# A decoder layer on one Trainium2 core: where the down weights are rounded, where the shared product is added, when the partition maximum is taken

## What is computed

```python
x = x + attn(layernorm(x))            # 16 heads of 32; int8 activations, ternary weights, causal softmax
x = x + xattn(layernorm(x))           # part two, below
x = x + ffn(layernorm(x))             # part two as well

# xattn, 32 heads of 8 positions; v = layernorm(x), x1 = x2 = context
kv  = v[:, :, i] * x2[:, :, j]        # an 8 x 8 outer product for every channel l
y   = causal_convolution(kv, k) + kv * skip          # along l = 512
out = sum over i of y[i, j] * x1[i]

# ffn, inner size 1536, weights rounded to float8 (e4m3) and back
fuse = silu((x @ q(gate_w)) * gate_scale) * ((x @ q(up_w)) * up_scale)
y    = (fuse @ q(down_w)) * down_scale
```

## Time and profile before

| | us |
|---|---|
| median of 3 runs | 1605.58 |
| their lowest and highest | 1601.24, 1606.38 |
| the profiled execution, its own time | 1601.21 |
| span of its trace, first to last instruction | 1599.4 |
| PE, DVE, POOL, ACT busy in the span | 1479.1, 1261.7, 992.7, 697.4 |

### The profile page before, as it was taken

How to read it: one execution, slowest core, us unless ns; L and a number is a source line. 1 busy time by engine, 2 the same in 40 slices (tenths; PEclk the granted TensorE clock), 3 DMA queues, 4 the chain that set the end, 5 groups by cost and what they waited for, 6 DMA issues and landing times.

```text
span 1599.4 us, 23982 instructions
## 1 busy us (share of the span) xinstructions
PE 1479.1 (92%) x8967; PEld 839.6 (52%) x9045; DVE 1261.7 (79%) x1841; ACT 697.4 (44%) x1222; POOL 992.7 (62%) x706
## 2 busy tenths in 40 slices
PE   2699999999876787999999999999999999999998
PEld 2477878888752333444444444444444444444443
DVE  5789999999855799888878787788778887878521
ACT  4589999999871103222222222322232223222231
POOL 2389999999973477456545654655645654566242
PEclk9799999999988999999999999999999999999999
DMA  3554645545315112000300210300030020010000
GB/s 135 154 138 132 175 136 148 159 145 144 100 59 184 42 50 77 22 7 14 79 14 9 72 27 0 79 21 7 20 80 7 14 79 14 7 40 1 1 26 27
DMA packets 58708, 105.78 MB, mean 66 GB/s; under 512 B 7625, under 2 KB 11873, under 8 KB 58593
## 3 DMA queue, kind: packets, MB, share of 16 engines
q1 hardware_dynamic: 58400, 104.10, 23.4%
q10 hardware_dynamic: 192, 0.14, 0.1%
HBM read 50.74 MB, written 19.92 MB: 44 GB/s over the span
## 4 chain that ended last, share of the span: by engine, by line
PE 61%; DVE 4%; POOL 2%; issue 1%; ACT 0%; POOLq 0%; DVEq 0%
PE gu L673 21%; PE y L638 10%; PE gu L687 10%; PE y L641 3%; PE y L646 3%; PE y L642 3%; PE gu L626 3%; PE y L645 3%; PE y L644 3%; PE misc L663 1%; PE misc L602 1%; PE misc L653 1%; PE misc L543 1%; DVE z L983 1%; DVE oT L994 1%
## 5 line engine op out<-in xcount | busy, mean ns | idle before, releaser
L1559 POOL TENSOR_TENSOR fuL<-fu,fuH 128x512 f16<-128x512 f32 x96 | 125.2, 1304 | 247.9 <-ACT fuH L1370 247.9
L638 PE MATMUL y<-kv,toep 128*128 128x512 f32 x496 | 239.8, 606 | 21.6 <-DVE z L983 19.2
L1465 POOL TENSOR_TENSOR pL<-pT,pH 128x768 f16<-128x768 f32 x128 | 216.6, 1694 | 10.9 <-ACT pH L1206 4.7
L994 DVE TENSOR_REDUCE oT<-z 128x64 f32<-128x512 f32 x256 | 175.7, 686 | 8.8
L673 PE MATMUL gu<-fT,wg 128*128 128x512 f16 x768 | 181.4, 379 | 0.3 <-ACT fT L1389 0.3
L673 PE MATMUL gu<-fT,wu 128*128 128x512 f16 x768 | 181.4, 379 | 0.0
L1370 ACT ACTIVATE fuH<-fu 128x512 f16<-128x512 f32 x96 | 60.3, 628 | 254.8 <-DVE fu L1009 254.8
L990 DVE TENSOR_TENSOR z<-z,cT 128x512 f32<-128x512 f32 x112 | 168.3, 1503 | 3.9
L987 DVE TENSOR_TENSOR z<-y,shared 128x512 f32<-128x512 f32 x112 | 76.9, 687 | 90.8 <-PE y L642 76.9
L687 PE MATMUL gu<-wd,fuH 128*128 128x512 f16 x384 | 145.5, 379 | 0.0
L687 PE MATMUL gu<-wd,fuL 128*128 128x512 f16 x384 | 145.5, 379 | 0.0
(11 more groups left out here) (188 smaller groups left out, 3392.3 us busy)
## 6 DMA issues: line engine op xcount, KB each, us to landing
pack<-qkhl SPq DMA_DIRECT2D x256, 128.0 KB, 2.4
x_sb<-in_x SPq DMA_DIRECT2D x16, 512.0 KB, 4.3
c_sb<-in_ctx SPq DMA_DIRECT2D x32, 256.0 KB, 5.0
hankel<-in_L_xattn_k SPq DMA_DIRECT2D x32, 256.0 KB, 4.4
x_grp<-x_scratch SPq DMA_DIRECT2D x32, 256.0 KB, 3.9
out_y<-yo SPq DMA_DIRECT2D x32, 256.0 KB, 2.8
x_scratch<-x_sb SPq DMA_DIRECT2D x15, 512.0 KB, 2.8
wraw<-in_L_attn_w_qkv SPq DMA_DIRECT2D x3, 1024.0 KB, 9.8
```

Source lines behind the costliest of these rows:

```text
L638: made = T.matmul(to, tap(h, lb - kb), keys_values(h, kb, half), start=kb == 0, stop=kb == lb)
L994: V.tensor_reduce(out=oT[h % 2][:, lb, own].rearrange("p (b j) -> p b j", b=HB), in_=z[n % 2][:], op=ALU.add, axis=AXIS.X).then_inc(m_z, 1)
L1465: G.tensor_tensor(pL[n % 2][:], pT[n % NP][:], pH[n % NP][:], ALU.subtract).then_inc(low_done, 1)
L1559: G.tensor_tensor(fuL[:, ib, :], fu[n % 2][:], fuH[:, ib, :], ALU.subtract).then_inc(f_fl, 1)
```

## The change

- The down weights are rounded in steps 33 to 56, one half tile in each step: DVE's pair in odd steps, POOL's in even ones. They get two raw buffers in place of three and memory of their own, and ACT's wait for them before `fuH` goes.
- The shared product is added to the PSUM bank in place, and one multiplication then goes from the bank to `z`, as in the other blocks. The bank is free after the multiplication, not after the addition.
- `weight_bound` goes to DVE's attention step 124, the partition maximum to POOL's attention step 142, one step after `sum_parts` of batch 15. `fuse_bound` stays in step 20.
- `sum_skip` goes from `s == 1` to `s == 3`, `spread_skip` from `s == 2` to `s == 4`.
- `hankel`, `v_sb` and `vT` have one buffer in place of two, `c_sb` two in place of three. So the taps of a head are loaded after ACT has turned those of the head before, and ACT writes `vT` after the products of the head before are done. SP loads the taps of head 1 after the first two loads of `x_grp`.

```diff
-        hankel = [q(f"hankel{i}", [P, L], F32) for i in range(2)]
+        hankel = q("hankel", [P, L], F32)
...
-        BOUND_AT = 6, 12, 20
+        FUSE_BOUND_AT = 20
...
+        WEIGHT_BOUND_AT, REDUCE_AT = (PIECES - 1) * PAIRS + CLAMP_AT + 1, (B - 1) * PAIRS + FINISH + 1
...
+        DOWN_AT = GROUP_STEPS
+
         def down_step(g):
 
-            k = (g - 2 * CB) * 3 // 4
-            return k if 1 <= k <= 2 * IB and (g - 1 - 2 * CB) * 3 // 4 < k else None
+            k = g - DOWN_AT
+            return k if 1 <= k <= 2 * IB else None
...
-                if h < SHARED_FROM or lb < 2:
-                    V.tensor_tensor(z[n % 2][:], y, weight, ALU.mult).then_inc(m_zm, 1)
-                    w.wait_ge(m_zm, n + 1)
-                else:
+                if h >= SHARED_FROM and lb >= 2:
                     w.wait_ge(m_shc, n_shared(h, half))
-                    V.tensor_tensor(z[n % 2][:], y, shared[half][:].rearrange("p (b j i) -> p b j i", b=HB, i=M_POS),
-                                    ALU.add).then_inc(m_zm, 1)
-                    w.wait_ge(m_zm, n + 1)
-                    chain.step(V.tensor_tensor(z[n % 2][:], z[n % 2][:], weight, ALU.mult))
+                    chain.step(V.tensor_tensor(y_bank[n % 2][:], y_bank[n % 2][:], shared[half][:], ALU.add))
                     chain.wait()
+                V.tensor_tensor(z[n % 2][:], y, weight, ALU.mult).then_inc(m_zm, 1)
+                w.wait_ge(m_zm, n + 1)
...
-                if s == 1 and h < M_HEADS:
+                if s == 3 and h < M_HEADS:
                     sum_skip(h)
...
-                if g == BOUND_AT[0]:
-                    weight_bound()
-                if g == BOUND_AT[2]:
+                if g == FUSE_BOUND_AT:
                     fuse_bound()
...
                 elif k == 3:
                     w.wait_ge(m_vtr, h + 1)
-                    if h >= 2:
-                        w.wait_ge(m_kv, 2 * (h - 1))
-                        w.wait_ge(m_kvp, 2 * (h - 1))
+                    w.wait_ge(m_kv, 2 * h)
+                    w.wait_ge(m_kvp, 2 * h)
...
+                if t == REDUCE_AT:
+                    w.wait_ge(mx_done, 1)
+                    G.partition_all_reduce(mall[:], mx[:], P, RMAX).then_inc(mall_done, 1)
...
             def load_taps(h):
-                if h >= 2:
-                    w.wait_ge(m_toep, h - 1)
+                w.wait_ge(m_toep, h)
...
-                if g == 2 * CB:
+                if g == DOWN_AT - 2:
                     down_load(0)
                     down_load(1)
-                if (k := down_step(g)) is not None and k % 2 == 1 and k // 2 + 2 < IB:
-                    down_load(k // 2 + 2)
+                if (k := down_step(g)) is not None and k % 2 == 0 and k // 2 + 1 < IB:
+                    down_load(k // 2 + 1)
```

More of the change, by code:

```diff
@@ L187, in decoder_kernel @@
         down_bc = q("down_bc", [P, C], F32)
-        c_sb = [q(f"c_sb{i}", [P, L], F32) for i in range(3)]
-        hankel = [q(f"hankel{i}", [P, L], F32) for i in range(2)]
+        c_sb = [q(f"c_sb{i}", [P, L], F32) for i in range(2)]
+        hankel = q("hankel", [P, L], F32)
         toep = [q(f"toep{i}", [P, L], F32) for i in range(2)]
@@ L193, in decoder_kernel @@
         x_grp = [q(f"x_grp{i}", [P, GROUP, C], F32) for i in range(3)]
-        v_sb = [q(f"v_sb{i}", [P, L], F32) for i in range(2)]
-        vT = [q(f"vT{i}", [P, LB, MT], F32) for i in range(2)]
+        v_sb = q("v_sb", [P, L], F32)
+        vT = q("vT", [P, LB, MT], F32)
         kv_skip = q("kv_skip", [P, LB * B, M_POS], F32)
@@ L213, in decoder_kernel @@
         fu = [q(f"fu{i}", [P, GN], F32) for i in range(2)]
-        with ExitStack() as down_prep:
-            d_raw = [sb(down_prep, f"d_raw{i}", [P, C], F32) for i in range(3)]
-            d_pow = [sb(down_prep, f"d_pow{i}", [P, C], F32) for i in range(2)]
+        d_raw = [q(f"d_raw{i}", [P, C], F32) for i in range(2)]
+        d_pow = [q(f"d_pow{i}", [P, C], F32) for i in range(2)]
         fuH = q("fuH", [P, IB, GN], F16)
@@ L601, in turn_v @@
                 for lb in range(LB):
-                    made = T.transpose(bank[:, lb * P:(lb + 1) * P], v_sb[h % 2][:, lb * P:(lb + 1) * P], ident[:])
+                    made = T.transpose(bank[:, lb * P:(lb + 1) * P], v_sb[:, lb * P:(lb + 1) * P], ident[:])
                 made.then_inc(m_vtr, 1)
@@ L870, in clamp_piece, with weight_bound @@
                                 accum_out=wmax[:, m, at:at + 1]).then_inc(fw_pow_done, 1)
+            def weight_bound():
+                chain.step(V.tensor_reduce(out=mx[:, 0:2], in_=wmax[:], op=ALU.max, axis=AXIS.X))
+                w.wait_ge(tab_done, 1)
+                chain.wait()
+                V.tensor_reduce(out=mx[:, 2:4], in_=cols[:, 0:2 * IB].rearrange("p (m b) -> p m b", m=2), op=ALU.max,
+                                axis=AXIS.X, apply_absolute_value=True).then_inc(mx_done, 1)
             stats_in(0)
@@ L931, in vector_program @@
                     clamp_piece(n)
+                if t == WEIGHT_BOUND_AT:
+                    weight_bound()
             scored(w)
@@ L1060, in down_weights @@
                     V.tensor_scalar(pw[:], pw[:], FP8_MIN_NORMAL, FP8_STEP, ALU.max, ALU.mult).then_inc(d_pow_done, 1)
-            def weight_bound():
-                chain.step(V.tensor_reduce(out=mx[:, 0:2], in_=wmax[:], op=ALU.max, axis=AXIS.X))
-                w.wait_ge(tab_done, 1)
-                chain.wait()
-                V.tensor_reduce(out=mx[:, 2:4], in_=cols[:, 0:2 * IB].rearrange("p (m b) -> p m b", m=2), op=ALU.max,
-                                axis=AXIS.X, apply_absolute_value=True).then_inc(mx_done, 1)
             def fuse_bound():
@@ L1336, in prepare @@
                     w.wait_ge(m_shift, h + 1)
-                    if h >= 2:
-                        w.wait_ge(m_vtr, h - 1)
-                    S.activation(v_sb[h % 2][:], xs, ACT.Identity, bias=sm[:, 9:10], scale=sm[:, 8:9]).then_inc(m_v, 1)
+                    w.wait_ge(m_vtr, h)
+                    S.activation(v_sb[:], xs, ACT.Identity, bias=sm[:, 9:10], scale=sm[:, 8:9]).then_inc(m_v, 1)
                     if h > 0:
@@ L1702, in sync_program @@
                     projected(w)
-                    for h in range(2):
-                        load_ctx(h)
-                        load_taps(h)
+                    load_ctx(0)
+                    load_taps(0)
+                    load_ctx(1)
             def load_x1(h):
```

47 lines of the change are left out of this document (21 added, 26 removed).

## The result

The changed kernel took 1589.95 us (median of 6 runs, 1585.76 to 1592.34), the kernel before 1604.18 beside it: 14.2 us less, ratio 0.991 with the interval 0.9893 to 0.9927. That is 0.9% faster, clear of the noise, and by the sum that was forecast. Whether the terms of the sum are right is another question, and most of this document is about it.

What follows compares the result with a forecast made beforehand. PE bounds the kernel from 640 us on; only its idle and half-clock time in heads 0 to 4 can be won. 7.6+1.7+2.4+1.2+2.3-0.5-0.5 = 14.2 us less gives a 1591 us median; range 1582 less 2 to 1602.

Steps and rivals of the forecast that it cites:

- The maximum: Head 2: moving the partition maximum away removes PE's 7.57 us stall, gain 7.6 us, and 1.7 us of slow clock after it.
- The half-clock term: 540 to 560 us, after head 2's gap: PE no longer runs at the lower clock, gain 1.7 us, at most 3.4.
- The skip sum: Moved two steps later: gain 2.4 us from head 0's wait, and 1.2 us from three small `v_sb` waits.
- The down weights out of heads 1 to 3: Heads 1 to 3: without DVE's pairs, a quarter of 9.2 us of other `z` waits goes, gain 2.3 us.
- Heads 4 to 6: Twelve down-weight pairs move into these heads: loss 0.5 us in head 4 and 0.5 us in heads 5 and 6.
- The addition in place: Addition to PSUM taken as 687 ns, multiplication 1503 to 683 ns; 0 from head 5 on, head 4's share within 0.5 us.
- Single buffers: Each single buffer adds a wait for taps or `vT`, but steps of some 4 us hide all of it: 0 us.
- The 6.95 us: Rival, chance 0.05: POOL's gap after the maximum has another cause and stays in head 2; gain 7.3 us, time 1598.
- Heads 5 and 6: Rival, chance 0.10: these heads give back 10 us in place of 0.5, leaving 4.7 us of gain, time 1601.
- More was not won: Rival that more is won, chance 0.14: DVE runs ahead of PE, nearly all `z` waits close, time 1582.
- the slower rival: Chance 0.07: POOL and DVE collide in the twelve moved pairs, each delaying a `z` PE needs; 18.9 us slower, time 1624.
- One sign of being wrong: Signs named: PE waits for `z` in heads 5 and 6, late power starting part two, PSUM addition far above 0.69 us.

## Why the prediction was right, and which steps of it were not

**The total** was right at 14.2 us, partly by luck: the terms below are off by several us in both directions, and 2.0 us of the 14.2 do not show in the part-two lengths of the two traces.

**The maximum (7.6 and 1.7 us).** Head 2 gained 8.45 us in the full change, idle 7.8 and busy 0.7. The size is near; the cause was read too narrowly. "POOL is late because of the partition maximum" leaves out 6.4 us that two down-weight tiles added in the same queue. With the pairs gone, moving the maximum is worth 0.5 us in the trace, because the wait behind `fuse_bound` covers it; with the pairs left, it is worth 4.5, because they then collide elsewhere. The half-clock term moved rather than went: the 20 slow matmuls behind `fuse_bound` are new.

**The skip sum (2.4 and 1.2 us)** was right: idle time in heads 0, 1 and 3 fell from 3.60, 1.39 and 2.06 us to 1.00, 1.07 and 1.32, 3.7 in all (0.42 of it is a `z` wait in head 3 that does not come back with this edit undone). With only this edit undone head 0 idles 3.64 us again, and the `v_sb` waits of heads 1 to 4 are 0.34, 0.34, 0.73 and 1.29 us, where the changed trace has one of 0.96: 2.6 and 1.7 us, on the paths that were named.

**The down weights out of heads 1 to 3 (2.3 us)** is the mis-sized step. I took only a quarter of the waits that were left once the other terms were out, and left out the clock. Nor were all of the 9.2 us the pairs' to give: 0.99 came before the first pair (PE at 521.56 us, the pair at 525.72) and 1.81 behind the last (632.09 us), which leaves 6.4. Put back, the pairs cost 6.2 us in these heads, 4.4 in PE's waits and 1.8 in clock.

**Heads 4 to 6 (losses of 0.5 and 0.5 us)** came out at a net loss of 0.3, where I had 1.0: head 4 gained 2.2, head 5 lost 2.4, head 6 lost 0.1. They come out near because two things that I priced apart offset each other: the pairs cost 5.2 us there alone, and the addition in place, which I put at nothing but a share of these losses, saves 4.2 with them.

**The addition in place.** The price of 687 ns measured 696. The Trainium skill's advice (VectorE: DVE Perf Modes, Rules for kernel authors) to copy out of PSUM first if many operations follow was rightly set aside here: 687 ns out of the bank against 1503 in SBUF. The 1503 is a mean beside a working POOL: in head 4 of before the same form took 0.69 us with POOL idle (at 612.04 us) and 2.12 us beside its `kv` (at 626.95 us).

**Single buffers (0).** No wait of PE in part two of the changed trace ends on `toep` or `vT`, and the one for `v_sb` is 0.96 us where 0.90 stood before; no run has them alone.

**The rivals.** The maximum was 11 us early at its new place. The 6.95 us were indeed not simply its own time, as the rival had it, but they did not stay ahead of head 2: every idle time of POOL there now ends on a result of DVE. Heads 5 and 6 gave back 2.5 us and not 10. More was not won: 18.1 us of idle PE are left, and `fuse_bound` stayed, as the prediction had against it; moving it brought 4.7 us more. Pairs collided, as the slower rival had it, the worst four at 2.6 to 3.3 us each, but in head 6 that no longer reached PE. One sign of being wrong did show: in head 5 PE waited for `z`, 1.35 us at 650.44.

## What to carry to other kernels

A stall that the chain of waits pins on one long instruction can belong to everything queued around it: before two edits are added up, ask whether they shorten the same queue, and test by undoing each from the whole as well as doing each alone. A delayed engine has several consumers, and freeing one of them, as `sum_skip` was, only shows the next. Small instructions of one engine are best put where the other engine that works on SBUF is idle, and off the short steps of the bound engine: the wait of 2.40 us there was followed by 1.6 us more of PE at its lower clock, though not in every run.

## What the runs showed of the hardware

- **Clock.** In heads 0 to 6 PE's busy time for the same matmuls went from 166.1 to 175.2 us between kernels. The difference comes in pieces behind short waits: 3.29 in place of 1.98 us for four matmuls, 7.01 in place of 5.32 for twelve, 10.63 in place of 9.04 for twenty. Not every wait of that length has one: 2.46 us in the earlier trace rows and 1.77 us in head 2 of the run with all but the skip sum had none.
- **DVE beside POOL.** Some instructions that work in SBUF alone take up to several times their time while POOL works: a pair's halves up to 1.74 and 2.06 us instead of 0.42 and 0.43, 1.87 instead of 0.16 for a 128x1 one, 2.17 instead of 0.69 for the addition to `oT`. Others don't: beside POOL's `kv` of 618.85 to 623.24 us of the changed trace the sum of `z` into `oT` takes 0.69 us and the statistics 0.68. The multiplication out of a bank stays at 0.68 to 0.69 us in the same rows.
- **The partition maximum** has 5.58 to 5.95 us without an instruction ahead of it in all 14 traces, wherever it stands. In the five with the maximum in part two another 6.95 to 7.38 us pass behind it; at the end of part one a memset right behind it did not pay them.
